# A DLRM tower on one core: dense inputs and layer-1 sums put into one 128-row operand, and layer 2's relu and addition moved one unit later

## What is computed

```python
e = jnp.stack([tbl_f[ids[:, f]] for f in range(32)], axis=1)      # (512, 32, 64)
# two layers: z[b, h*32+f, d] = hidden[b, h, d] * x[b, f, d]
y = jnp.einsum('bcd,oc->bod', z, w) + b[None, :, None]             # 128 outputs
y = relu(y)          # layer 1: first 64 are the next hidden, last 64 are output; layer 2: all 128 are output
z = jnp.concatenate(finals, axis=1).sum(-1)                        # (512, 192)
h = jnp.concatenate([z, dense_ctx], axis=1)                        # (512, 208)
h = jnp.maximum(h @ W_top1 + b_top1, 0.0)                          # 512 wide
h = jnp.maximum(h @ W_top2 + b_top2, 0.0)                          # 256 wide
y = h @ W_top3
```

## Time and profile before

| what | value |
|---|---|
| median of three runs | 1107.88 us (1106.35 to 1109.63) |
| the profiled execution | 1107.58 us |
| its span in the trace | 1105.8 us |
| TensorE busy | 1036.2 us, 94% |
| VectorE busy | 943.5 us, 85% |
| GpSimd busy | 914.6 us, 83% |
| ScalarE busy | 738.2 us, 67% |
| granted TensorE clock, mean | 0.974 |

### The profile page before, as it was taken

One profiled execution on the slowest core, in us unless ns is written; L12 is line 12 of the kernel. 1 busy time (PEld: TensorE's weight loads), 2 busy tenths in 40 slices (PEclk: granted clock), 3 DMA queues, 4 the chain that ended last, 5 costly groups with the idle time before them and its releaser, 6 DMA issues.

```text
span 1105.8 us, 10714 instructions
## 1 busy us (share of the span) xinstructions
PE 1036.2 (94%) x3501; PEld 651.5 (59%) x3501; DVE 943.5 (85%) x621; ACT 738.2 (67%) x907; POOL 914.6 (83%) x300
## 2 busy tenths in 40 slices
PE   1059999999999999999999999999999999999999
PEld 1025556666666666666666566666666666666652
DVE  3059999999999999999999999999889988889860
ACT  1046656767777677777777677777777777777741
POOL 7526778879899999999999899998988898888950
PEclk9569999999999999999999999999999999999998
DMA  4287777777878778787887788777887778877610
GB/s 134 51 195 192 193 187 184 187 195 189 198 192 202 181 194 208 181 200 188 206 199 183 187 197 209 185 198 185 194 204 184 188 184 199 198 184 189 157 39 0
DMA packets 142073, 196.89 MB, mean 178 GB/s; under 512 B 15857, under 2 KB 57457, under 8 KB 141890
## 3 DMA queue, kind: packets, MB, share of 16 engines
q1 hardware_dynamic: 137922, 192.01, 70.2%
q0 software_dynamic: 4096, 4.20, 1.7%
HBM read 175.18 MB, written 20.97 MB: 177 GB/s over the span
## 4 chain that ended last, share of the span: by engine, by line
PE 87%; POOL 3%; DVE 3%; DMA 3%; issue 2%; ACT 2%; SPq 1%; DVEq 0%; ACTq 0%
PE py L606 39%; PE py L622 15%; PE py L612 15%; PE py L613 14%; POOL emb L292 3%; DVE zf L494 2%; DMA xs<-x_dram 1%; ACT zh L361 1%; PE py L627 1%; DMA x_dram<-xf 1%; PE pt L588 1%; DVE zl L511 1%; SPq L260 0%; PE hid L635 0%; PE py L672 0%
## 5 line engine op out<-in xcount | busy, mean ns | idle before, releaser
L302 POOL TENSOR_TENSOR zl<-zf,zh 128x2048 fp32r<-128x2048 f32 x168 | 771.5, 4609 | 121.4 <-ACT zh L361 120.2
L494 DVE TENSOR_TENSOR zf<-xs,hid 128x2048 f32<-128x2048 f32 x256 | 578.8, 2280 | 58.0 <-ACT hid L376 55.4
L606 PE MATMUL py<-zf,wf 128*128 128x512 f32 x1072 | 485.0, 595 | 6.3 <-DVE zf L494 6.3
L361 ACT ACTIVATE zh<-zf 128x2048 fp32r<-128x2048 f32 x186 | 354.5, 1906 | 12.1 <-DVE zf L494 11.8
L606 PEld LDWEIGHTS py<-zf,wf 128*128 128x128 f32 x1072 | 202.9, 190 | 214.6 <-issue 194.0
L612 PE MATMUL py<-zh,wh 128*128 128x512 f32 x744 | 294.3, 396 | 9.4 <-ACT zh L361 9.4
L613 PE MATMUL py<-zh,wl 128*128 128x512 f32 x744 | 292.5, 393 | 0.0
L622 PE MATMUL py<-zl,wh 128*128 128x512 f32 x744 | 234.5, 437 | 1.0 <-POOL zl L302 1.0
L494 DVE TENSOR_TENSOR zf<-xs,px 128x2048 f32<-128x2048 f32 x64 | 146.4, 2288 | 40.1 <-DMA xs<-x_dram 38.2
L622 PEld LDWEIGHTS py<-zl,wh 128*128 128x128 f32 x744 | 135.6, 189 | 61.1 <-issue 33.5
L612 PEld LDWEIGHTS py<-zh,wh 128*128 128x128 f32 x744 | 140.3, 189 | 47.0 <-ACT zh L361 13.5
(11 more groups left out here) (74 smaller groups left out, 450.3 us busy)
## 6 DMA issues: line engine op xcount, KB each, us to landing
xs<-x_dram SPq DMA_DIRECT2D x640, 256.0 KB, 4.4
x_dram<-xf SPq DMA_DIRECT2D x64, 320.0 KB, 3.5
emb<-in_tbl,idx POOLq DMA_INDIRECT x128, 4.1
xs<-in_L_rec_w SPq DMA_DIRECT2D x2, 512.0 KB, 4.7
xs<-in_L_rec_w SPq DMA_DIRECT2D x1, 1024.0 KB, 7.3
wt<-in_W_top SPq DMA_DIRECT2D x1, 512.0 KB, 7.3
wt1b<-in_W_top SPq DMA_DIRECT2D x1, 256.0 KB, 6.5
wt1a<-in_W_top SPq DMA_DIRECT2D x1, 128.0 KB, 6.5
```

The costliest lines, as they stand in the source:

```text
L302: pool.tensor_tensor(zl[:, q], zf[:, s], zh[:, q].bitcast(F32), ALU.subtract).then_inc(lo["P"], 1)
L361: act.activation(zh[:, q], zf[:, s], ACT.Copy).then_inc(hi, 1)
L494: dve.tensor_tensor(zf[:, slot(u)], left, right, ALU.mult).then_inc(mult, 1)
L606: mm = pe.matmul(y, wf[:, w, h], zf[:, s, h], start=first and h == 0, stop=ends and h == T - 1)
```

## The change

Three things are done.

1. The 16 dense rows move into the same operand as the 64 layer-1 rows. `zd` has 128 rows: 0 to 15 dense, 16 to 63 zero, 64 to 127 the layer-1 sums. `wt1a` gets the 16 dense rows of `W_top1` on partitions 0 to 15 and zeros on 16 to 63. `top_1_begin` is then one matmul over 128 rows in place of one over 16 and one over 64. Layer 2's sums lie in `zsum2`.
2. For the zeros VectorE runs two memsets (64 x 512 each) first of all, and counts them in `cleared`. The load of the 16 weight rows waits for `cleared` and stands last of SyncE's 15 loads at the start.
3. `finish_2(g-1)` stands behind `high` C on ScalarE, and `add_2(g-1)` stands behind products B on VectorE.

```diff
@@ operands @@
-        zsum = sb("zsum", [P, 2, B])
+        zd = sb("zd", [P, B])
+        zsum2 = sb("zsum2", [P, B])
...
-        wt1c = sb("wt1c", [16, B])
...
-        denseT = sb("denseT", [16, B])
@@ SyncE @@
-            sp.dma_start(wt1c[:], W_top1[H + P:H + P + 16, :]).then_inc(top_in, 16)
...
+            sp.wait_ge(cleared, 2)
+            sp.dma_start(wt1a[0:16, :], W_top1[H + P:H + P + 16, :]).then_inc(top_in, 16)
@@ ScalarE, each group @@
+                high(("C", g))
                 if g >= 1:
                     finish_2(g - 1)
-                high(("C", g))
                 if g + 3 < G:
                     copy_xf(g + 3)
@@ VectorE, start @@
+            dve.memset(wt1a[0:H], 0.0).then_inc(cleared, 1)
+            dve.memset(zd[0:H], 0.0).then_inc(cleared, 1)
...
-            dve.tensor_copy(denseT[:], px0[0:16]).then_inc(s_low, 1)
+            dve.wait_ge(cleared, 2)
+            dve.tensor_copy(zd[0:16], px0[0:16]).then_inc(s_low, 1)
@@ VectorE, sum_d @@
-                dve.tensor_reduce(zsum[rows, a, P * c:P * c + P], acc[rows, c % 2].rearrange("p (d b) -> p b d", d=ND),
+                dve.tensor_reduce((zd, zsum2)[a][rows, P * c:P * c + P], acc[rows, c % 2].rearrange("p (d b) -> p b d", d=ND),
@@ VectorE, each group @@
+                products(("B", g))
                 if g >= 1:
                     add_2(g - 1)
-                products(("B", g))
                 low(("C", g))
                 products(("D", g))
@@ TensorE, top network @@
-                pe.matmul(top1[m], wt1c[:, cols], denseT[:], start=True, stop=False)
-                pe.matmul(top1[m], wt1a[H:P, cols], zsum[H:P, 0], start=False, stop=False)
+                pe.matmul(top1[m], wt1a[:, cols], zd[:], start=True, stop=False)
...
-                pe.matmul(top1[m], wt1b[:, P * m:P * m + P], zsum[:, 1], start=False, stop=True).then_inc(top_mm, 1)
+                pe.matmul(top1[m], wt1b[:, P * m:P * m + P], zsum2[:], start=False, stop=True).then_inc(top_mm, 1)
```

More of the change, by code:

```diff
@@ L178, in dlrm_tower @@
         gathered = [sem("gathered%d" % c) for c in range(NC)]
-        w_doubled, w_turned = sem("w_doubled"), sem("w_turned")
+        cleared, w_doubled, w_turned = sem("cleared"), sem("w_doubled"), sem("w_turned")
         w_high, w_low, s_low, dense_turned = sem("w_high"), sem("w_low"), sem("s_low"), sem("dense_turned")
```

## The result

The changed kernel takes **1092.14 us** (median of 4 runs, 1091.28 to 1092.62), the kernel before 1107.38 (4 runs, 1106.35 to 1109.63). The ratio is 0.9868, 95% interval 0.9854 to 0.9882. The forecast was 1095.3 with a range down to 1092.8: the sign is right, and most of the gain comes where it was forecast. The gain is 15.2 us where 12.6 were forecast, and the time lies 0.7 us under the range; as a ratio the forecast was 0.9886, just outside the interval too. The profiled execution took 1092.62 us.

What follows compares the result with a forecast made beforehand. TensorE, busy 94% of the span, was taken as the bound, with most to win in the top network and group 63. Gains 7.66 + 2.47 + 2.1 + 0.4 = 12.6 us gave 1095.3 us against the median, range 1092.8 to 1099.0.

Steps and rivals of the forecast that it cites:

- (a): Top network, first matmuls: eight 128-row passes over `zd` replace 16 narrow ones, 11.09 us becoming 3.43, a gain of 7.66 us.
- (b): Top network, second matmuls: eight passes at full instead of half clock, 5.90 us becoming 3.43, a gain of 2.47 us.
- (c): Group 63: TensorE's waits for GpSimd's remainder of A and ScalarE's `zh` of C go, gain 2.1 us, bounds 0 and 2.9.
- (d): Groups 1 to 62: the moved relu and addition give back little, 0.4 us, bounds 0 and 1.5.
- the 15.7 us of waits: Groups 1 to 62: all the time additions wait for relus, claimed to be VectorE's and not TensorE's.
- (e): The start: two VectorE memsets and the late load of 16 weight rows lie off the path, 0 us.
- the 3.06 us gather: The start: a GpSimd gather beside VectorE's copies at 10 to 13.6 us took 3.06 us against 1.09 for the first.
- The order gave more than forecast, not nothing: Rival for groups 1 to 63: the new order gives nothing, (c) and (d) at 0, 1097.8 us; chance 0.08.
- The slower case: Rival: VectorE's addition waits for `finish_2`, delaying remainder of C and products D; 1135.6 us at 1 us lateness; chance 0.03.
- the 0.4 us of cover: Nearly every group: the relu ends about 2.5 us after C's products, VectorE reaches the addition 2.9 us after them.
- the first rival: Top network: the clock falls all the same, at 1081.4, costing 5.1 us and giving 1100.4 us; chance 0.09.

Runs made afterwards that it cites:

- order_only: The kernel before with only the moved relu (`finish_2`) and addition (`add_2`), without the padded operand: 1103.60 us, ratio to before 0.9971.
- add_only: The kernel before with only VectorE's addition (`add_2`) moved behind products B, ScalarE's relu left in place: 1106.22 us, ratio to before 0.9995.
- sums_moved: The changed kernel with the two accumulator sums moved out of groups whose C is V (18 and 33) into 19, 34 and 35: 1091.03 us.
- zero_passes: The changed kernel with 32 further passes over all-zero operands, four matmuls behind each matmul over `zd`: 1105.59 us.
- relu_only: The kernel before with only ScalarE's relu (`finish_2`) moved behind the rounding of C, VectorE's addition left in place: 1202.58 us, ratio to before 1.0862.
- top_only: The changed kernel with relu and addition of layer 2 back in their old places, padded operand kept: 1096.61 us, ratio to before 0.9905.
- copies_on_act: The changed kernel with the weight preparation's twelve copies at the start moved from VectorE to ScalarE: 1091.38 us, ratio to before 0.9868.

## Why the prediction was right, and where it was wrong

**(a) and (b), the top network: right, to the tenth.** 10.13 us forecast, 10.12 in the trace. The pass over `zd` has the 0.429 us that was taken; the clock stays up; the last sum was ready at 1075.57, 0.95 us before the passes that need it, where 0.9 us of cover was forecast:

```profile
1074.54 1.03 DVE L544 TENSOR_REDUCE zsum<-acc 128x128 f32<-128x512 f32 x1
```

**(c), group 63: right.** 2.1 us forecast, 2.2 measured. Timeline of VectorE, ScalarE and GpSimd after, beside the earlier trace rows:

```profile
1046.14 1.92 ACT L362 ACTIVATE zh<-zf 128x2048 fp32r<-128x2048 f32 x1 [1.59 <-DVE zf L498]
1048.08 0.66 ACT L392 ACTIVATE py<-py,bias 128x512 f32<-128x512 f32 x1
```

```profile
1048.13 13.74 POOL L303 TENSOR_TENSOR zl<-zf,zh 128x2048 fp32r<-128x2048 f32 x3 [0.69 <-ACT zh L362]
```

```profile
1058.47 2.29 DVE L498 TENSOR_TENSOR zf<-xs,hid 128x2048 f32<-128x2048 f32 x1 [0.73 <-DMA xs<-x_dram]
1063.27 0.69 DVE L539 TENSOR_TENSOR acc<-py,acc 128x512 f32<-128x512 f32 x1 [2.51 <-ACT py L392]
1063.88 2.28 DVE L515 TENSOR_TENSOR zl<-zf,zh 128x2048 fp32r<-128x2048 f32 x1
1066.08 2.28 DVE L498 TENSOR_TENSOR zf<-xs,hid 128x2048 f32<-128x2048 f32 x1
```

C(62) is rounded ahead of the relu, GpSimd's three remainders follow at once and end at 1061.87, 0.7 us before late B(62) is done; the prediction had both end together. Products B now wait 0.73 us for a load, a wait that the prediction didn't have, and it costs nothing, since the addition behind them waits 2.51 us anyway. Products D end at 1068.36; main D starts at 1065.29 + 3.43 = 1068.72, so the cover is 0.36 us (0.3 forecast).

**(d), groups 1 to 62: this step failed.** Forecast 0.4 us, upper bound 1.5, measured 1.6 (1.9 by the means of the traces with either order). The step that failed is the sentence that the 15.7 us of waits "are VectorE's, not TensorE's: moving them gives back little". It held for the gaps that the prediction counted, the ones of half a microsecond and more. But in the groups behind those whose C is V (from 18 to 36), VectorE is late, products B come last, and TensorE waits 0.1 to 0.2 us for their rounding. The first pass of main B(22) before and after (TensorE, timeline):

```profile
435.02 0.40 PE L613 MATMUL py<-zh,wl 128*128 128x512 f32 x1
435.33 0.50 PE L612 MATMUL py<-zh,wh 128*128 128x512 f32 x1
435.67 0.39 PE L613 MATMUL py<-zh,wl 128*128 128x512 f32 x1
```

```profile
433.56 0.39 PE L617 MATMUL py<-zh,wl 128*128 128x512 f32 x1
433.79 0.39 PE L616 MATMUL py<-zh,wh 128*128 128x512 f32 x1
434.02 0.39 PE L617 MATMUL py<-zh,wl 128*128 128x512 f32 x1
```

The steps from start to start are 0.31 and 0.34 us before, 0.23 after: 0.19 us regained. Before, products B stood behind the addition, at 431.05 us, and ScalarE rounded them from 433.36 to 435.28, so the first pass of main B came at 435.33. After, they stand ahead of the addition, at 428.66, and the rounding ends at 433.33, before TensorE is there at 433.79. No idle time is noted there, since a matmul's row is 0.39 us long and spans the gap. There are seven such places, main B of groups 19, 22, 25, 28, 31, 34 and 37, and together they give back 1.1 us of the missing 1.2 (`order_only` and `add_only` gain it at the same seven, so it is the order's). Of the 0.4 us that was forecast, group 1 gave its 0.2. Before groups 19 and 34 the gaps went, from start to start, from 0.71 to 0.74 us and from 0.96 to 0.85: one of the two tenths came. `sums_moved` shows that the sum makes what is left of them.

**(e), the start: 0 forecast, 1.0 us in the trace, by all that is known chance.** The memsets took 0.48 us each and ended at 1.93 us, before the first gather, as forecast, and six of the nine traces with memsets have the start of the kernel before. What was put at nothing is that the start varies between executions: the first embedding copy comes at 46.6 to 49.1 us. The prediction named the 3.06 us gather and left the range without it.

**The rivals.** The clock did not fall, and `zero_passes` shows that zeros don't make it. The order gave more than forecast, not nothing. The slower case did not come, but `relu_only` shows how near it lies: the 0.4 us of cover that stood against it exist only because both instructions moved.

**The sum and the range.** The profiled execution was forecast at 1094.95 us and took 1092.62. The trace explains these 2.3 us: 1.2 by (d), 1.0 by the start, 0.1 by (c). (d) alone would have left the time in the range. The median lies another 0.5 us lower, and which start its runs had no trace shows, so the last 0.7 us below the range can't be told from scatter. By the medians of single experiments, `order_only` gave 3.4 us (2.5 forecast) and `top_only` 10.4 (10.1 forecast), 13.9 in all, and 1107.0 − 13.9 = 1093.2 us would lie in the range; the changed kernel gained 15.2. The interval of its ratio, 13.1 to 16.2 us, takes in both, so no run shows a gain beyond the two parts.

Two slips stand in the working and change nothing above. The fall of the clock at 1083.3 came 5.4 us behind the first narrow pass at 1077.92, not 5.6, so the first rival's fall would come at 1081.2. And the range was drawn narrower than its own parts: the bounds of (a) to (d) reach from 1093.4 to 1098.5 us, not 1097.8, and with the ±1.7 us of a median the lower end would have been 1091.7, which takes in the result.

## What to carry to other kernels

Make the last small matmuls as tall as those around them: zero rows cost TensorE nothing here, while narrow matmuls among them cost 0.2 us at every change of height and, where all of a stretch were narrow, 10 us at half the clock. When an instruction that waits moves on one engine, move its consumer on the next engine by the same distance, or the wait can grow into a circle through both engines, at 1.5 us a group here. And on a pipelined TensorE look for waits in the distance from start to start, since a row's length hides those under 0.2 us, and many small ones add up. Where a stretch varies between executions, as the start does here, let the range take it in.

## What the hardware showed that was not expected

- Unbroken work does not keep the clock. `order_only`, without the padding, loses it again, with TensorE busy in every moment of the 4 us shown and of the 400 us ahead of them:

```profile
1080.00:1084.00 4.00, 4.00 (x5) 0.99 (x4) 0.00 (x0) 0.00 (x0) 0.00 (x0) 0.50 0.00 0
```

- Passes over all-zero operands, 32 of them, with 8 others, in 17 us, run at the full clock.
- VectorE's copies hold GpSimd's gathers up: beside VectorE's work at the start a gather takes 1.4 to 3.3 us, 0.94 otherwise, and with the copies on ScalarE all but one take 0.94 to 1.1. The addition among them seems to do it too: in the kernel before it runs from 13.60 to 14.67, beside a gather of 1.50 us, and in `copies_on_act` beside the one of 1.63. Which gathers are held up changes from execution to execution.
